# Group 0 of a ternary FFN: the down product from plain quarters instead of a seven-product scheme

## What is computed

```python
def ternary_quant(w):
    scale = jnp.mean(jnp.abs(w)) + EPS
    q = jnp.clip(jnp.round(w / scale), -1.0, 1.0) * scale
    return w + jax.lax.stop_gradient(q - w)
wu = ternary_quant(W_up)      # 2048 x 512
wg = ternary_quant(W_gate)    # 2048 x 512
wd = ternary_quant(W_down)    # 512 x 2048
up = jnp.einsum('bsd,ed->bse', x, wu)
gate = jnp.einsum('bsd,ed->bse', x, wg)
hidden = jax.nn.silu(up) * gate
return jnp.einsum('bse,de->bsd', hidden, wd)
...
x = x + 0.5 * _L0_ffn_ref(_layernorm(x, axis=-1), ...)
```

## Time and profile before

| | us |
|---|---|
| median of 3 runs (1897.47 to 1900.08) | 1899.9 |
| the profiled execution | 1898.84 |
| its span, first to last instruction | 1897.1 |
| PE busy | 1785.2 (94%) |
| DVE busy | 1390.7 (73%) |
| POOL busy | 868.2 (46%) |
| granted TensorE clock, mean | 0.992 |

### The profile page before, as it was taken

The page is one execution under the profiler, slowest core; times in us unless marked ns, Lnnn a source line. Parts: engine busy times, 40 slices in busy tenths (PEclk is TensorE's granted clock), DMA queues, the critical chain, the costliest instruction groups (busy, mean ns, idle before and its releaser), DMA issues. The chain is left out here.

```text
span 1897.1 us, 35095 instructions
## 1 busy us (share of the span) xinstructions
PE 1785.2 (94%) x13046; PEld 1261.5 (66%) x13046; DVE 1390.7 (73%) x2325; ACT 919.7 (48%) x1381; POOL 868.2 (46%) x583
## 2 busy tenths in 40 slices
PE   5779899999999899999999999899999999999998
PEld 2354688888888764444444444454788888888887
DVE  6977877877775656796796797756787777877654
ACT  5324374574653635444444444424365474564552
POOL 1898452442533514454454355545253352442533
PEclk9899999999999999999999999999999999999999
DMA  7021203113114021111112111110321212112100
GB/s 310 1 44 47 62 28 80 39 44 83 39 44 134 2 74 38 36 49 61 37 46 61 38 45 39 56 61 6 84 40 45 61 36 69 39 44 61 39 23 23
DMA packets 132330, 102.89 MB, mean 54 GB/s; under 512 B 100752, under 2 KB 100752, under 8 KB 130448
## 3 DMA queue, kind: packets, MB, share of 16 engines
q1 hardware_dynamic: 132240, 101.77, 18.0%
HBM read 49.59 MB, written 25.17 MB: 39 GB/s over the span
## 5 line engine op out<-in xcount | busy, mean ns | idle before, releaser
L436 POOL TENSOR_TENSOR f_hlo<-f_h,f_hhi 128x768 f16<-128x768 f32 x144 | 220.3, 1530 | 643.6 <-ACT f_hhi L572 629.9
L1007 PE MATMUL f_down_ps<-wd,f_hhi 128*128 128x256 fp8e4 x1536 | 342.1, 274 | 15.1 <-POOL f_hlo L436 11.0
L1007 PE MATMUL f_down_ps<-wd,f_hlo 128*128 128x256 fp8e4 x1536 | 342.1, 274 | 0.0
L1048 PE MATMUL f_gate_ps<-spare 128*128 128x256 f16 x2496 | 307.5, 273 | 4.9 <-issue 4.3
L1048 PEld LDWEIGHTS f_gate_ps<-spare 128*128 128x128 fp8e4 x2496 | 237.1, 98 | 46.9 <-issue 5.9
L1048 PE MATMUL f_up_ps<-spare,wu 128*128 128x256 f16 x1664 | 216.7, 273 | 1.3 <-issue 1.1
L770 DVE SCALAR_TENSOR_TENSOR xa<-f_down_ps,out_scale,xa 128x512 f32<-128x512 f32 x208 | 145.5, 744 | 93.1 <-PE f_down_ps L1007 92.4
L1007 PEld LDWEIGHTS f_down_ps<-wd,f_hhi 128*128 128x128 f16 x1536 | 150.9, 98 | 38.8 <-issue 20.5
L1048 PEld LDWEIGHTS f_up_ps<-spare,wu 128*128 128x128 fp8e4 x1664 | 160.7, 98 | 23.7 <-issue 2.1
L436 POOL TENSOR_TENSOR f_hlo<-late,f_hhi 128x1024 f16<-128x1024 f32 x76 | 166.6, 2192 | 2.2 <-ACT f_hhi L578 2.2
L1007 PEld LDWEIGHTS f_down_ps<-wd,f_hlo 128*128 128x128 f16 x1536 | 151.0, 98 | 17.9
(11 more groups left out here) (216 smaller groups left out, 3256.9 us busy)
## 6 DMA issues: line engine op xcount, KB each, us to landing
res<-xa SPq DMA_DIRECT2D x16, 1024.0 KB, 4.3
xa<-res SPq DMA_DIRECT2D x16, 1024.0 KB, 5.4
xa<-in_u SPq DMA_DIRECT2D x8, 1024.0 KB, 5.2
xa<-res SPq DMA_DIRECT2D x32, 256.0 KB, 2.6
res<-xa SPq DMA_DIRECT2D x32, 256.0 KB, 2.0
spare<-in_w_up SPq DMA_DIRECT2D x4, 1024.0 KB, 10.2
late<-in_w_gate SPq DMA_DIRECT2D x4, 1024.0 KB, 17.6
late<-in_w_in SPq DMA_DIRECT2D x1, 2320.0 KB, 8.7
```

Source lines behind the costliest of these rows:

```text
L436: last = nc.gpsimd.tensor_tensor(hlo[:, p, a:b, :], src, hhi[:, p, a:b, :], ALU.subtract)
L1007: last = nc.tensor.matmul(at, part[:, p, kind, m * P:(m + 1) * P], wd[:, weight, p, :], start=(p == 0 and part is hhi), stop=(p == HK - 1 ...
L1048: last = nc.tensor.matmul(acc[:, j * HT:(j + 1) * HT], w[:, k, e * P:(e + 1) * P], xop[part][:, o, k, :, :], start=(fresh and (j, k, part) ...
```

## The change

In group 0 the down product is computed directly. `direct_group` of each engine takes the place of `group(0, between)`, and `group` keeps only what group 1 needs. No sums of h are made in group 0: ACT copies the four quarters in one operation of 1024 elements, POOL makes the low part in two operations of 512 elements. PE works by tiles of 128 tokens (`down_tile_of`): 8 pairs, 2 halves of the hidden units, 2 parts, 2 halves of the output, which is 64 matmuls of 256 columns for each of 4 tiles, 256 in all. Tiles 0 and 1 run over pairs 0 to 6, then over pair 7, then tiles 2 and 3; tile 0 waits for both low parts of every pair up to 6, and tiles 2 and 3 wait until DVE has added the tile two before in the same bank. DVE adds 4 tiles of 512 columns and normalizes group 1's tokens ahead of all of them. The sums of the down weights stay behind POOL's pair 7 and are read by group 1 first. POOL's `inv_std(1)` moves from pair 4 to pair 5. Counters of sums (`sum_step`) start 32 further on.

```diff
                 done_before = ((norm_done, CH), (xnh_done, CH), (xnl_done, CH), (turned, 32))
-                if not first:
+                if first:
+                    done_before += ((sum_step, 4 * HK),)
+                else:
...
+                def down_tile(t):
+                    return after(t + 1 if t < CH - 1 else 7)
...
                         eng.wait_ge(hlo_done[1], after(HK // 2 * g))
-                        if first:
-                            eng.wait_ge(tern_done, 1 + max(n for n, v in enumerate(TERNARY) if v[:2] == (1, 0)))
...
-                        def group(g, between=None):
+                        def direct_group():
                             for p in range(HK):
-                                if first and p == 5:
+                                if p == 5:
+                                    inv_std(1)
                                     pool.wait_ge(tern_done, 2 + AT_DOWN[0])
-                                if first and p == HK - 1:
+                                if p == HK - 1:
                                     pool.wait_ge(tern_done, N_TERN)
-                                if between is not None and p < HK - 1:
-                                    pair_sums(pool, nc.gpsimd, g, p)
...
+                                for n in range(2):
+                                    pool.wait_ge(hhi_done, after(2 * p + n + 1))
+                                    nc.gpsimd.tensor_tensor(hlo[:, p, 2 * n:2 * n + 2, :], h[:, p % 2, 2 * n:2 * n + 2, :],
+                                                            hhi[:, p, 2 * n:2 * n + 2, :], ALU.subtract)\
+                                      .then_inc((hla_done, hlo_done)[n][p % 2], 1)
+                            t_sums()
+                            for i in range(S_EARLY):
+                                s_sum(i)
...
+                        def hid_high_direct(p):
...
+                            nc.scalar.activation(hhi[:, p, 0:4, :], h[:, p % 2, :, :], ACT.Copy).then_inc(hhi_done, 2)
...
+                        def direct_group(between):
+                            for i in range(KE):
+                                hidden(0, i)
+                                between(i)
...
+                            for c in (0, 2):
+                                normalize_rows(1, c, c + 2)
+                                low_rows(1, c, c + 2)
+                            for t in range(CH):
+                                dve.wait_ge(down_done, down_tile(t))
...
+                                nc.vector.scalar_tensor_tensor(dst, down_ps[:, D * (t % 2):D * (t % 2 + 1)], out_scale[:, 0:1],
+                                                               dst, ALU.mult, ALU.add)\
...
-                            for name in ORDER:
-                                add_product(g, name)
-                                if name in ("P1", "P3"):
...
+                        def down_tile_of(t, p0, p1):
+                            if p0 == 0 and t > 1:
+                                pe.wait_ge(res_done, after(t - 1))
+                            if t == 0:
+                                for p in range(p0, p1):
+                                    pe.wait_ge(hla_done[p % 2], after(p // 2 + 1))
+                                    pe.wait_ge(hlo_done[p % 2], after(p // 2 + 1))
+                            pe.wait_ge(tern_done, N_TERN)
+                            for p in range(p0, p1):
+                                for upper in range(2):
+                                    kind = 2 * (t // 2) + 1 - upper
+                                    for part in (hhi, hlo):
+                                        for j in range(2):
+                                            w = (b12 if j else wd[:, 0, :, :], wd[:, 2 if j else 1, :, :])[upper]
...
+                        def direct_group(between):
+                            for i in range(KE):
+                                if i > 3:
+                                    up_gate(0, i)
+                                between(i)
+                            for t in range(2):
+                                down_tile_of(t, 0, HK - 1)
+                            for t in range(2):
+                                down_tile_of(t, HK - 1, HK)
+                            for t in range(2, CH):
+                                down_tile_of(t, 0, HK)
```

More of the change, by code:

```diff
@@ L473, in group @@
                                 low_parts(g, p, 1, sums[0])
[L474 to L476 removed]
+                                if p == HK - 1:
                                     inv_std(g + 2)
[L478 removed]
+                                if first:
                                     s_sum(S_EARLY + p)
                             if first:
[L481 removed]
+                                for i in range(S_EARLY + HK, 16):
                                     s_sum(i)
@@ L562, in _ @@
                                     abs_sum(w, q)
+                        def hid_high_direct(p):
+                            if p == 3:
+                                act.wait_ge(abs_done, 12)
+                            if p == HK - 1:
+                                act.wait_ge(tern_done, N_TERN)
+                            for half in range(2):
+                                act.wait_ge(hid_done[half], after(p + 1))
+                            nc.scalar.activation(hhi[:, p, 0:4, :], h[:, p % 2, :, :], ACT.Copy).then_inc(hhi_done, 2)
                         def hid_high(g, p):
-                            if first and p == 3:
-                                act.wait_ge(abs_done, 12)
-                            if first and p == HK - 1:
-                                act.wait_ge(tern_done, N_TERN)
                             for half in range(2):
@@ L1035, in group @@
+                        def group(g):
+                            for i in range(KE):
+                                up_gate(g, i)
                             down(g, 0, False)
@@ L1144, in _ @@
                             weight_sum(0)
-                            group(0, last_sum)
+                            direct_group(last_sum)
                         group(NC - 1)
```

91 lines of the change are left out of this document (44 added, 47 removed).

## The result

The kernel after takes 1878.4 us (median of four runs, 1870.6 to 1880.6), the one before 1898.7 us in the same series: a ratio of 0.989, with a 95% interval of 0.987 to 0.991. The two later series give 0.9877 [0.9861, 0.9894] and 0.9884 [0.9867, 0.9900]. The profiled execution of after took 1870.56 us, its span is 1868.9 us.

A forecast was written before the change was run, and what follows sets the result against it. PE bounds nearly everywhere, but DVE, held up 21.5 us by POOL, sets group 0's up/gate stage. Gains 10.2 + 3.7 - 1.1 = 12.8 us take the median from 1899.9 to 1887.1, range 1880 to 1896.

The forecast's parts named there:

- The sharing by busy time: Alternative to whole-instruction turns between DVE and POOL: POOL's remaining 15.8 us would cost DVE 5.6 us instead of 8.9.
- Part 1: Group 0's up/gate stage up to `hidden` of block 13: 19.1 us go, 8.9 stay, gain 10.2 us (3.3 to 12.6).
- 1.5 us a pair: Cost to DVE of POOL's two remaining low-part operations: 0.4 us on one ternary piece, 1.1 us on the next.
- Part 2: From `hidden` of block 13 to PE's first down product: 5.2 us instead of 8.9, waiting for POOL; gain 3.7 us.
- Part 3: Group 0's down product, 256 matmuls for 224: 29.0 us instead of 27.9, a loss of 1.1 us.
- the half of the low clock: In the down product, 0.9 us kept of the 1.7 us that some 16 matmuls at the lower clock cost before.
- Part 4: POOL's weight sums before group 1's low parts: the 2.7 us of slack grows; worth nothing, costs nothing.
- The rival that the weight sums wouldn't move ahead: POOL's weight sums do not begin earlier but keep their place behind pair 7; this changes no number. No chance given.
- The rival of an almost free DVE: POOL's two operations fall under `hidden`, statistics and DVE's waits: 23 us gained, 1877 us; chance 8%.
- The range's upper gain of part 1: Upper bound up to `hidden` of block 13: 13 POOL operations at 0.5 us cost 6.5 us, gain 12.6.
- unchanged pieces: Group 0's ternary pieces stay slow, or another limit holds the stage: only 2.6 us gained, 1897.3 us; chance 13%.
- slow clock: PE runs the longer down product at its lower clock; loses from 132 of 256 matmuls, 1912.8 us with all; chance 4%.

The follow-up runs named there:

- c3_after: The kernel after, unaltered, run again on the chip of e7_split and e8: 1879.2 us, ratio 0.9884.
- e1_no_sums: The kernel before with group 0's sums of h left out on POOL and DVE; copies, low parts and seven products stay: 1889.8 us, ratio 0.9947.
- e2_sums_back: The kernel after with four unused POOL additions of 256 elements behind the low parts of each of pairs 0 to 6: 1881.8 us, ratio 0.9909.
- e3_fills_back: The kernel after with four POOL fills of 256 elements behind the low parts of each of pairs 0 to 6: 1878.7 us, ratio 0.9885.
- e6_low_one: The kernel after with a pair's two low parts of 512 elements made as one POOL operation of 1024: 1879.7 us, ratio 0.9895.
- e7_split: The kernel after with tile 0 taking low parts pair by pair and waiting for the last two ternary pieces only at pair 4: 1875.4 us, ratio 0.9866.
- e5_late_stats: The kernel after with group 1's statistics and variance moved behind group 0's last `hidden`, POOL's pow behind pair 7: 1878.4 us, ratio 0.9877.
- e4_seven_plain: The kernel before with group 0's low parts and copies as in after, no sums, seven products from plain quarters: 1876.9 us, ratio 0.9881.
- e8: The kernel after with both the changed waits of e7_split and the later statistics of e5_late_stats: 1876.5 us, ratio 0.9866.
- c2_before: The kernel before, unaltered, traced a second time: 1896.4 us in its one execution.
- c1_after: The kernel after, unaltered, run again: 1875.8 us, ratio 0.9877.

## Why the prediction was right or wrong

**What bounds.** Right. The stage is DVE's, the excess lay in the ternary pieces, and what goes there reaches the end: in the first trace of after the lead at the transfers behind group 0 is 18.8 us and never less afterwards (in c3_after it falls to 17.8 for a while). e1_no_sums and e2_sums_back show the cause from both sides: fewer POOL operations in the kernel before gave 7.6 us, more in the kernel after took 4.1.

The section of the Trainium skill that the prediction quotes ("SBUF — State Buffer", "SBUF: two separate sides", an exclusive lock for a whole instruction) agrees with these rows: pieces are held or not held, by 0.24 and 0.78 us, and run at 0.75 and 1.28 us otherwise; nothing is slowed in proportion. What is held is less than the POOL instruction's recorded 1.15 us. The sharing by busy time that stood against it in the prediction (5.6 us kept where the turns gave 8.9) was nearer in number to the 5.1 us measured, but not by its mechanism.

**Part 1: the direction right, the size wrong.** 15.9 us came for 10.2. The term that failed is the 8.9 us that POOL was to cost DVE up to h13, 5 x 1.5 + 0.4 + 1.0. It measures 5.1 us:

- "1.5 us a pair", 0.4 + 1.1, is 0.24 + 0.78 = 1.02 in pairs 0, 3, 4 and 5, 0.48 less in each and 1.9 us less together. Laid out, the prediction had taken the whole of POOL's 1.15 us as time in which DVE is held. It isn't: where a piece lay fully behind a POOL operation it lost 0.78 us, and where `hidden` hid the first 0.66 us it lost 0.24, so 512 elements hold DVE for 0.8 to 0.9 us, and the rest of the recorded 1.15 us lies beside it.
- Pair 1 cost 0.17 for 1.5, since it fell beside the statistics. In e3_fills_back and e6_low_one, where DVE is 0.7 us later at this point, the pair meets a piece instead, so the 1.3 us gained here are in part luck.
- The variance's `pow`, priced at 1.0 us, cost nothing; it fell beside a piece that was already held.
- Pair 2, at the weight scale, cost 0.9 for 0.4.

Together these are 3.8 of the 5.7 us missed. What goes was sized right: 18.7 us of excess and 0.4 at the scale are the 19.1 of the prediction. But DVE also waited 1.7 us for silu in this stretch, and no longer does. The prediction had named that wait and given it no price. 19.1 + 1.7 - 5.1 is 15.7, and the 0.2 left of the 15.9 lie in no row.

**Part 2: the number nearly right, by the wrong cause.** 3.1 us for 3.7, a wait of 5.8 us for 5.2. The prediction's step was that PE waits for POOL's second low part, at 5.0 us. The rows say DVE's last piece, L937, which ended with a POOL turn in it (2.06 us for 1.28), while POOL's two operations of pair 6 were through 1 us earlier:

```profile
91.59 2.06 DVE L937 SCALAR_TENSOR_TENSOR wd<-xa,half,f_hlo 128x1024 fp8e4<-128x1024 f32 x1
```

```profile
89.26 3.31 POOL L477 TENSOR_TENSOR f_hlo<-f_h,f_hhi 128x512 f16<-128x512 f32 x2 [4.97 <-ACT f_hhi L585]
```

The change's own `pe.wait_ge(tern_done, N_TERN)` stands in the diff that the prediction quotes, and DVE's order has the last piece just ahead of block 15's `hidden`; following it would have given the cause. e7_split agrees: with that wait two pieces later, and the low parts taken up pair by pair, the 2.0 us are gone.

**Part 3: too pessimistic by 1.0 us.** The down stage took 28.1 us for 27.9, a loss of 0.15 us against 1.1. 256 x 0.109 = 27.9 and the 0.2 for tile 2 were right; the half of the low clock was not met. It was in reach, as e5_late_stats shows (29.8 us, the 0.9 us and more). The other half of the calculation was right, too: e4_seven_plain puts seven products at 26.3 us at full clock, 1.8 less than the direct product, and the 1.6 us that before lost beside that are the low clock in the earlier trace rows. The wait for a bank is none of them, since e4_seven_plain has one too, 1.68 us for 1.32.

**Part 4: right.** POOL's sums begin 23 us earlier, the slack grew to 7.1 us, and group 1's stage is as long as it was (1.0 us longer in c3_after, at the low clock). The rival that the weight sums wouldn't move ahead is refuted, and as said it changes no number.

**The sum.** Group 0 gives 18.8 us where 12.8 were forecast: +5.7, -0.6 and +1.0. The rival of an almost free DVE, with 19.1 + 5.3 - 1.1 = 23, had the better number and was half right: the pieces stand at 41.8 us, below the 42 that the prediction had named as its mark. DVE is not free, 4.2 us of excess remain, but the turns that remain fall half under `hidden` and in pair 1 under the statistics, which is the reason that rival gave. The range's upper gain of part 1, 12.6, was drawn from the average of 0.5 us an operation, where the 13 measured 0.4 each, and it left out DVE's own wait of 1.7 us.

**The range.** It was missed by 1.6 us, and not by group 0 alone: 18.8 us taken from the 1899.9 that the prediction started from are 1881.1, which lies inside. Of the 2.7 us down to 1878.4, 1.2 are the median of before, 1898.7 with a fourth run, and 1.5 lie behind group 0, where no run places them.

The rivals of unchanged pieces and of a slow clock are refuted.

**What stays open.** The medians of after gain 20.4, 24.3 and 22.2 us in the three series, group 0 only 18.8. The eight kernels e1 to e8 show the same sign: their medians gain 2.3 to 4.9 us more than their group 0 does. Single traces don't show it: against c2_before the traces of the later kernels end ahead by more than their group 0 gives in some cases and by less in others, and two executions of one kernel differ by 2.4 us. Nor does the mean granted clock: it is 0.989 to 0.994 over before's runs and 0.993 to 0.997 over after's, and group 0 with its 0.90 and 0.95 in the earlier trace rows, 1.00 now, accounts for about that difference. The traces do show one loss that is not in every execution: in group 1 the lead falls by about 1 us in c3_after, e4, e5, e6 and e8, and not in after, c1_after, e3 and e7. Of the medians' gain 1.5, 5.4 and 3.3 us have no place yet. Whether the new group 0 changes what the later stages meet, or the runs without a profile differ in another way, the runs don't tell.

## What to carry to other kernels

Where DVE bounds a stage and POOL works beside it, count for each POOL operation which DVE operation it meets and whether that one is held: here `hidden`, which reads PSUM, was not, and a POOL turn that falls under it is nearly free. Fewer turns pay first, and two short ones can beat a long one, since one of them may fall under such a cover. When a wait is about to go, read in the changed code every other wait of the same instruction, for the one that is next: here that wait, moved together with the one for the low parts, was worth 2.2 us.

## What was not expected of the hardware

- A POOL operation's recorded span is longer than the time in which it holds DVE: 128x512 f32 is recorded with 1.15 us undisturbed and held a piece for 0.78 us, 128x1024 with 2.34 us held one for 1.75 us.
- Four fills of 128x256 take 1.06 us on POOL and four additions of the same size 3.7 to 4.7 us beside DVE; over the 24 of each up to h13 the stage grew by 1.5 and 4.1 us. Fills ran beside a compare-and-subtract with neither of the two held (four pairs of e3_fills_back), but held a compare by 0.74 us (1.73 for 0.99).
- Very short DVE operations are held too: a 128x1 operation of the weight scale took 1.02 us for 0.16 beside a POOL turn. `hidden` kept its 0.72 to 0.75 us and the statistics their 1.28 for two in the same stage.
- The granted clock of later stages isn't a property of the program: two traces of the kernel before agree to 0.02 us over the first 140 us, and then have their low spells in different places, 2.4 us apart at the end.
- After the same 2.03 us of idle time PE kept the full clock in three traces (after, c1_after, c3_after), and in e5_late_stats, where the stage before was 1.6 us shorter, ran eleven matmuls at full clock and then 16 at 1.2 GHz. After 2.29 and 2.23 us of idle time (e2_sums_back, e6_low_one) the clock stayed full as well.
